# 64-wide attention: which unit's reciprocal DVE takes ahead of each unit's maximum

## What is computed

```python
h = _rms(x, ln_w)
q = (h @ wq).reshape(B, S, NHEADS, HEAD_DIM)   # 32 query heads of 64
k = (h @ wk).reshape(B, S, KVHEADS, HEAD_DIM)  # 8 key heads, each for 4 query heads
v = (h @ wv).reshape(B, S, KVHEADS, HEAD_DIM)
q, k = _rope(q, k)
...
scores = jnp.einsum('bqhd,bkhd->bhqk', q, k) / np.float32(np.sqrt(HEAD_DIM))
scores = jnp.where(causal[None, None], scores, jnp.float32(-1e+30))
attn = jax.nn.softmax(scores, -1)
o = jnp.einsum('bhqk,bkhd->bqhd', attn, v).reshape(B, S, NHEADS * HEAD_DIM)
x = x + o @ wo
```

## Time and profile before

| | us |
|---|---|
| median of three runs | 2093.55 (2091.25 to 2094.47) |
| profiled execution, its own time | 2085.89 |
| its span, first to last instruction | 2084.1 |
| from the first to the last full maximum of the 64-wide attention | 828.9 to 1707.4 |
| one round of it in the middle | 27.79 |

### The profile page before, as it was taken

The page is one execution under the profiler, slowest core; times in us unless marked ns, Lnnn a source line. Parts: engine busy times, 40 slices in busy tenths (PEclk is TensorE's granted clock), DMA queues, the critical chain, the costliest instruction groups (busy, mean ns, idle before and its releaser), DMA issues.

```text
span 2084.1 us, 32302 instructions
## 1 busy us (share of the span) xinstructions
PE 1797.1 (86%) x10666; PEld 1216.7 (58%) x10666; DVE 1289.7 (62%) x3898; ACT 1072.1 (51%) x2854; POOL 903.1 (43%) x1013
## 2 busy tenths in 40 slices
PE   4989899868888864999999999999999984799994
PEld 2656678733334323677766677767666764555552
DVE  5675555445775855777777777777777766522222
ACT  3323344225565542666666666666666661344442
POOL 3992000102212001555555555555555552588884
PEclk9999999957999996999999999999999995899997
DMA  5000020000001010000000000000000008255556
GB/s 154 1 1 1 1 61 1 1 0 1 1 1 41 1 44 0 1 1 2 1 1 1 1 1 1 1 1 1 1 1 1 1 1 289 64 84 84 82 84 167
DMA packets 61426, 61.71 MB, mean 30 GB/s; under 512 B 13136, under 2 KB 58320, under 8 KB 61264
## 3 DMA queue, kind: packets, MB, share of 16 engines
q0 software_dynamic: 15360, 20.98, 6.3%
q1 hardware_dynamic: 45904, 38.65, 5.8%
HBM read 40.48 MB, written 19.14 MB: 29 GB/s over the span
## 4 chain that ended last, share of the span: by engine, by line
PE 56%; DVE 21%; issue 9%; ACT 8%; POOL 4%; DMA 2%; SPq 0%; POOLq 0%; ACTq 0%; DVEq 0%
PE banks L1813 6%; PE banks L1804 5%; PE banks L1773 4%; PE banks L1795 4%; PE banks L1783 4%; DVE wide_x L1052 3%; PE banks L1990 3%; PE banks L1867 3%; PE banks L1617 3%; PE banks L1825 2%; POOL wdT L725 2%; PE banks L1842 2%; DVE con L1063 2%; PE banks L1679 2%; PE banks L1887 2%
## 5 line engine op out<-in xcount | busy, mean ns | idle before, releaser
L1773 PE MATMUL banks<-wide_k,wide_q 128*128 128x512 f32 (+3 forms) x1024 | 307.2, 382 | 4.6 <-DVE con L1037 1.9
L1406 ACT ACTIVATE wugT<-wugT,con 128x512 f32<-128x512 f32 (+1 forms) x256 | 170.5, 667 | 136.2 <-DVE con L1037 136.1
L657 POOL TENSOR_TENSOR wugT<-wugT,con 128x512 f32<-128x512 f32 (+1 forms) x256 | 232.8, 935 | 2.5 <-DVE con L1016 2.5
L668 POOL TENSOR_TENSOR attn<-attn 128x320 f32<-128x320 f32 x128 | 111.4, 870 | 248.7 <-DVE attn L1004 248.7
L1037 DVE CUSTOM_DVE_ANT_0 wugT<-banks,wide_mask 128x512 f32<-128x512 f32 (+1 forms) x256 | 158.0, 617 | 98.7 <-PE banks L1773 94.8
L1773 PEld LDWEIGHTS banks<-wide_k,wide_q 128*128 128x128 f32 x1024 | 166.8, 190 | 59.1 <-DVE con L1037 24.0
L1063 DVE TENSOR_REDUCE con<-banks 128x1 f32<-128x512 f32 x256 | 163.6, 681 | 57.4 <-PE banks L1855 57.0
L1813 PE MATMUL banks<-late,attn 128*128 128x384 f32 x512 | 189.4, 493 | 2.0 <-DVE attn L1009 1.2
L1795 PE MATMUL banks<-attn 128*64 128x256 f32 x1280 | 166.4, 389 | 0.0
L1990 PE MATMUL banks<-w,late 128*128 x320 | 158.2, 618 | 2.2 <-issue 1.2
L1237 DVE TENSOR_TENSOR late<-late,banks 128x256 f32<-128x256 f32 x80 | 33.7, 422 | 197.6 <-ACT late L1539 168.3
(11 more groups left out here) (310 smaller groups left out, 4148.2 us busy)
## 6 DMA issues: line engine op xcount, KB each, us to landing
w<-in_L_ffn_w_dram SPq DMA_DIRECT2D x32, 256.0 KB, 6.1
late<-in_L_ffn_w_dram SPq DMA_DIRECT2D x16, 256.0 KB, 6.2
y_rows<-wqkv1T SPq DMA_DIRECT2D x1, 2176.0 KB, 7.9
x<-in_L_attn_x_dram SPq DMA_DIRECT2D x4, 512.0 KB, 9.3
late<-in_L_ffn_wq_dram SPq DMA_DIRECT2D x2, 1024.0 KB, 7.2
late<-in_L_ffn_wo_dram SPq DMA_DIRECT2D x1, 2048.0 KB, 9.2
h_rows<-wugT SPq DMA_DIRECT2D x1, 2048.0 KB, 7.0
y_rows<-x SPq DMA_DIRECT2D x1, 2048.0 KB, 13.1
```

What stands on the lines that cost most here:

```text
L657: nc.gpsimd.tensor_tensor(p, p, rinv[:, m:m + 1].to_broadcast([P, n]), ALU.mult).then_inc(at.sem["norm"], 1)
L1406: nc.scalar.activation(at.prob(m)[:, 0:n], at.prob(m)[:, 0:n], ACT.Exp, bias=negmax[:, m:m + 1], scale=-1.0, accum_out=rowsum[:, m:m + 1]) ...
L1773: ins = nc.tensor.matmul(sbank[:, 0:keys], wide_q[:, side, i, qcols], wide_k[:, side, w, 0:keys], start=(w == 0), stop=(w == 1))
```

## The change

The eighth argument of `Attention` is `behind`. It becomes 1.

```diff
-        a2 = Attention("a2", [(r, 0) for r in reversed(range(TB))], HD64, True, wide_bufs, 10, 2, 2, WIDE)
+        a2 = Attention("a2", [(r, 0) for r in reversed(range(TB))], HD64, True, wide_bufs, 10, 2, 1, WIDE)
```

## The result

| | us |
|---|---|
| before, median | 2094.01 (2091.25 to 2096.33) |
| changed kernel, median | 2183.7 (2178.14 to 2187.82) |
| ratio | 1.0439, 95% interval 1.041 to 1.0468 |
| forecast | 2168 (2138 to 2215) |

The changed kernel is slower by 90 us. The profiled execution took 2178.14 us, against 2085.89 before.

A forecast was written before the change was run, and what follows sets the result against it. PE was taken as the bound, busy 26.66 of 27.79 us a round; DVE's new waits for ACT add 2.4 a round, 31 x 2.4 = 74, on 2093.55: 2168 us, range 2138 to 2215.

The forecast's parts named there:

- The lateness step by step: DVE's maxima in one round: each waits for the previous unit's exponential sum plus 0.12; late 0.38 at unit 1, 2.73 at unit 10.
- the rival in which the gaps swallow nothing: DVE's idle gaps of 0.18 and 0.47 stay: 2.9 to 3.4 us a round, 2184 to 2199 us; chance 0.13.
- PE's share: DVE's lateness of 2.73 at unit 10 reaches PE at unit 12's scores; a round grows 2.2 to 2.7, 2.4 taken.
- The 0.31 read at the scores of unit 12: PE's scores of unit 12 already waited 0.31 us for unit 10's maximum, so no cover was left there.
- The 0.53 that PE might have saved: PE's own later stop before a turn of queries and keys, saved if ACT keeps up, leaving 2.2 a round.
- two cases: PE's 0.53 stop is saved, 2.2 a round, or ACT behind unit 12's exponential keeps it, 2.7.
- The 0.38 for POOL's sooner multiplications: PE's turns wait for POOL 0.38 us a round; sooner multiplications could gain at most that, 12 us in all.
- As a rival it stood at 0.9 us a round: POOL gets out of the way of DVE's slow low subtractions: 1.5 a round remains, about 2140 us; chance 0.09.
- The rival had 0.93 and 62 us: PE's granted clock falls to 0.93, its work takes 2.0 longer a round, about 2230 us; chance 0.08.
- wrong below 0.98: Sign against the forecast: PE's granted clock in the rounds of the 64-wide attention lying below 0.98.
- 88% against stretches at 81 and 84%: PE's busy share expected in a round, against earlier stretches with clock 1.00 at 81% and 0.93 at 84%.

The follow-up runs named there:

- the kernel with slot 4 alone: Kernel before, with the reciprocal one unit back at slot 4 only and two back elsewhere, POOL too: 2131.25 us, ratio 1.0204.
- two kernels: Changed kernel with POOL two units back everywhere, 2139.85 us; changed kernel with POOL's multiplications of units 3 and 6 one slot later, 2142.71 us.
- kernels with rounds of 29.93 and 29.3 us: Changed kernel with unit 3's exponential ahead of slot 3's high copies on ACT, 2160.26 us; changed kernel with POOL deferring units 3 and 6, 2142.71 us.

## Why the prediction came out as it did

**What bounds.** Right: PE sets the round before, with no cover where the new waits stand, and the change turns DVE into the bound from unit 4 to unit 12.

**The lateness step by step.** Predicted, and measured in a short round against the start of unit 0: unit 1, 0.38 and 0.37 (1349.22 - 1347.56 = 1.66 against 1.29); unit 3, 0.20 and 0.10; unit 4, 1.36 and 1.31; unit 6, 2.04 and 2.04; unit 7, 3.17 and 3.18; unit 8, 2.43 and 2.29; unit 9, 3.20 and 3.04; unit 10, 2.73 and 2.47. Small terms were swallowed a little better than worked out. Unit 8's 2.29 behind unit 7's 3.18 also settles the rival in which the gaps swallow nothing.

**PE's share.** The sum was 2.2 to 2.7, 2.4 taken; 2.45 measured. The figure held, but one reason was incomplete, and part of the fit is luck. I let all of it reach PE at the scores of unit 12. In fact PE stops first at unit 7's scores and its output product, 0.97 and 0.39, and the kernel with slot 4 alone shows that this way by itself costs 1.24. The way over unit 10 adds the rest. The 0.31 read at the scores of unit 12 was idle time of the weight loads alone; PE's matmuls had no stop there. The 0.53 that PE might have saved it did not save, and the lateness at unit 10 was 2.47 and not 2.73: the 2.4 lay between two cases of which neither came, and the two errors nearly cancel.

**The gain.** The 0.38 for POOL's sooner multiplications was no price at all. In the changed kernel nothing waits for POOL there, and the weight loads of the turns stand idle as long as before (12.3 us then):

```profile
PEld banks L1783 <- issue: 12.8, 33, 0.5
```

PE's own matmuls had no stop at this place, before or after. The kernel before gains 0.2 a round when a multiplication comes later.

**POOL.** As a rival it stood at 0.9 us a round for the "low" pairs, with a chance of 0.09 that the change brings it. The mechanism is real, and 0.93 was measured in two kernels, but that the size agrees is luck: it was argued from the pair of 1.40, which is 1.39 to 1.40 in both of them still, and the 0.93 comes from the pairs of slots 4 and 7. The change does not bring it either: by tying the multiplication to the reciprocal before units 4 and 7 it keeps both collisions (1.16 and 1.01, where they took 1.10 and 0.96). The Trainium skill ("SBUF — State Buffer", section "SBUF: two separate sides") says that DVE with two inputs in SBUF and GpSimd hold a shared port in turns, each for a whole instruction. What was measured when one of the two is moved away agrees with it, 0.62 for 1.16.

**The clock.** This is the term that failed: the forecast of 2168 put it at nothing. The rival had 0.93 and 62 us; it was 0.96 on average behind the first round and 14.8 us, and with it the time is 2184 and not 2168. The forecast said it would be wrong below 0.98, and by that mark this part was. I had compared mean shares of busy time, 88% against stretches at 81 and 84%. That did not tell it: kernels with rounds of 29.93 and 29.3 us keep 1.00 behind the first round, with stops of 0.65 and 0.43 at the same place. The Trainium skill ("TensorE: Matmul & The Clock Gate", section on psum-queue depth-cycling) describes such swings from short idle times between groups; the two kinds of round agree with it. What lets the clock fall in two rounds of three and not in the third, behind the same stops of 0.97 and 0.39, stays open.

## What to carry to other kernels

Before tying an engine in order to another one's result, work out for each place when that result ends and what is queued behind the wait: here twelve of sixteen waits cost 0.1 us a round together, and one of the other four made half the cost. A semaphore that releases work on POOL also decides which DVE instruction it runs beside, and moving one multiplication by a slot gained 0.2 us a round where the edit studied lost 2.45. A stop of a microsecond on PE, once a round, can cost more than its length through the clock (here another 0.74 in two rounds of three), and work without a purpose put into it can pay. A wait named in the profile is a price only where the engine's real work stands still: two idle times of weight loads were priced here, 0.31 and 0.38, at places where the matmuls had no stop.

## What the runs showed of the hardware

- A pair of DVE subtractions with both operands in SBUF takes 0.62 us alone, and 1.16, 1.45 or up to 1.80 beside POOL's multiplications. POOL's own multiplication gets longer too at times, 1.14 in place of 1.04.
- With a stop of PE of 0.97 us and one of 0.39 behind it in each round of 30.2 us, the granted clock fell in 20 of the 30 rounds behind the first, to 0.70 over the next 5.71 us. With the first stop at 0.45, 0.65 or 0.43 it did not fall in any of these 30. In the kernel with slot 4 alone the stops were 0.86 and 0.39, and it did not fall either; the length of the stop alone is thus no full account, and what else counts was not settled.
- Six turns of 128x128 on PE in a place where PE waits anyway cost nothing.
